# Attention scores in four groups of 32 rows on four PSUM banks, row maxima from the f32r tiles, another order of a step

## What is computed

```python
# layer 0: 16 heads of 16
Q = x @ Wq + bq
KV = text_input @ Wkv + bkv
scores = einsum('bqhd,bkhd->bhqk', Q, K) * 0.25
out = einsum('bhqk,bkhd->bqhd', softmax(scores, axis=-1), V)
# layer 1: 8 heads of 32
scores = einsum('bqhd,bkhd->bhqk', qh, kh) / 16
oh = qh + einsum('bhqk,bkhd->bqhd', softmax(scores, axis=-1), vh)
O = layernorm(oh); O = O + relu(O @ Wo.T + bo); O = layernorm(O)
```

## Time and profile before

| | us |
|---|---|
| median of 3 runs | 2231.89 |
| lowest, highest | 2225.58, 2285.02 |
| the profiled execution | 2223.33 |
| its span | 2221.6 |
| PE busy in the span | 1721.6 (77%) |
| DVE busy | 1030.7 (46%) |
| POOL busy | 1033.6 (47%) |
| ACT busy | 896.1 (40%) |

### The profile page before, as it was taken

The page is one execution under the profiler, slowest core; times in us unless marked ns, Lnnn a source line. Parts: engine busy times, 40 slices in busy tenths (PEclk is TensorE's granted clock), DMA queues, the critical chain, the costliest instruction groups (busy, mean ns, idle before and its releaser), DMA issues. The chain is left out here.

```text
span 2221.6 us, 45766 instructions
## 1 busy us (share of the span) xinstructions
PE 1721.6 (77%) x14350; PEld 1272.6 (57%) x14351; DVE 1030.7 (46%) x2291; ACT 896.1 (40%) x1823; POOL 1033.6 (47%) x1421
## 2 busy tenths in 40 slices
PE   5888888888864999958777777777775268888884
PEld 4666666666643666646666565656664135555552
DVE  3555555555534222224555555554455724444442
ACT  3666666666641222225444444444442011111110
POOL 4656666666631111134544555454543036666663
PEclk8999999999986999978989999999997589999998
DMA  4111111000014111120111111100000222222223
GB/s 111 41 46 59 44 63 44 26 26 19 20 31 163 33 33 33 33 73 12 51 40 61 47 48 41 48 23 27 25 23 12 94 80 36 38 38 38 38 38 81
DMA packets 54163, 102.08 MB, mean 46 GB/s; under 512 B 11842, under 2 KB 37674, under 8 KB 50698
## 3 DMA queue, kind: packets, MB, share of 16 engines
q1 hardware_dynamic: 37754, 78.87, 11.0%
q0 software_dynamic: 16352, 22.47, 5.5%
HBM read 79.78 MB, written 24.93 MB: 47 GB/s over the span
## 5 line engine op out<-in xcount | busy, mean ns | idle before, releaser
L950 DVE TENSOR_REDUCE a_mx<-a_SM 100x2 bf16<-100x722 f32 x384 | 350.2, 912 | 351.1 <-PE a_SM L423 349.2
L1533 PE MATMUL e_PH<-w,e_xT 128*128 x712 | 326.5, 602 | 6.0 <-DVE e_ab L1665 2.9
L695 ACT ACTIVATE a_Pr<-a_ST 120x800 f32<-120x800 f32 (+1 forms) x288 | 241.8, 854 | 46.6 <-PE a_ST L459 46.4
L423 PE MATMUL a_SM<-a_KTb,a_QMb 64*100 64x361 bf16 x768 | 136.9, 353 | 133.2 <-DVE a_mx L950 131.0
L745 POOL TENSOR_TENSOR a_rstd<-a_ve,a_powers 100x1 f32<-100x1 f32 x192 | 117.4, 611 | 223.2 <-DVE a_ve L919 223.1
L1533 PEld LDWEIGHTS e_PH<-w,e_xT 128*128 128x128 f32 x712 | 134.8, 193 | 141.4 <-issue 138.6
L1454 POOL COPY e_gidx<-toks 128x1 int32 (+1 forms) x89 | 48.6, 546 | 300.2 <-PE e_PX L1522 206.7
L470 PE MATMUL a_M<-a_Pr,a_V 120*32 120x100 f32 (+3 forms) x4608 | 186.6, 262 | 0.3 <-ACT a_Pr L695 0.3
L423 PEld LDWEIGHTS a_SM<-a_KTb,a_QMb 64*100 64x100 bf16 x768 | 47.0, 119 | 225.8 <-DVE a_mx L950 187.1
L1619 ACT ACTIVATE e_hT<-e_PT 128x512 f32<-128x512 f32 x57 | 34.0, 597 | 332.7 <-PE e_PY L1556 309.2
L452 PE MATMUL a_ST<-a_MXM,a_ones_bf 64*120 64x400 bf16 (+1 forms) x576 | 104.1, 357 | 68.3 <-POOL a_MXM L833 67.1
(11 more groups left out here) (194 smaller groups left out, 4038.2 us busy)
## 6 DMA issues: line engine op xcount, KB each, us to landing
w<-in_E_w SPq DMA_DIRECT2D x24, 1024.0 KB, 5.9
a_ct<-in_ctx SPq DMA_DIRECT2D x64, 362.0 KB, 3.2
keep_rows<-a_keep SPq DMA_DIRECT2D x64, 100.0 KB
tile_rows<-e_y SPq DMA_DIRECT2D x32, 128.0 KB
b_rows<-in_E_b SPq DMA_DIRECT2D x1, 4096.0 KB
sums<-X SPq DMA_DIRECT2D x1, 3200.0 KB
out<-sums SPq DMA_DIRECT2D x2, 1600.0 KB, 9.4
X<-in_x SPq DMA_DIRECT2D x1, 2800.0 KB
```

The source lines that it names most:

```text
L423: last = nc.tensor.matmul(SM[0:LQ, half, 0:LK], QMb[rows, chunk, m, :], KTb[rows, chunk, :], start=True, stop=True)
L695: nc.scalar.activation(dst.rearrange("p (j q) -> p j q", j=2), ST[0:n, (b.p * NS + s) % 2, :, 0:4 * LQ], ACT.Exp, scale=SCALE).then_inc(ex ...
L950: V_.tensor_reduce(pair, SM[0:LQ, :, 0:LK], AX_X, ALU.max).then_inc(max_done, 1)
L1533: last = nc.tensor.matmul(PH[:, h, :], xT[:, c, :], rhs, start=(c == 0), stop=(c == DC - 1))
```

## The change

- `ROWS` is 32 in both layers. In layer 0 HT becomes 2, in layer 1 it becomes 1: no mask and no spreading. There QM is written by ScalarE from the queries (in the place of q_hi), QL by GpSimd as queries minus QM, and MXM is the copy of the maxima that ScalarE makes.
- A slot is a key tile with all heads: three slots in both layers. Its products run over four row groups, each with its own bank of `ST`, which has four banks and one buffer. Slot s waits for the exponential of slot s-1. In layer 0 ScalarE's exponential is one instruction of 1600 columns.
- `score_rows` multiplies QM and KT; KTb and QMb with their copies are gone, and KF, KT and KL are 362 wide.
- The product with V runs by key tile (three blocks of all heads) and not by head group (four blocks of three tiles).
- In layer 1 the query rows are transposed from qf instead of being projected again.
- The order of a step changes on four engines: the front's first half stands ahead of the transposed maxima; VectorE's `tail1a` and `tail1c` stand ahead of all reduces; GpSimd's `power(2)` moves from ahead of the gather to the next step's start.

```diff
-TILE_ROWS = (64, 64)
+ROWS = 32
+GROUPS = 128 // ROWS
...
-        MXM = sb("MXM", [128, DC, HT, LQ], BF16)
+        MXM = sb("MXM", [128, DC, HT, LQ], BF16) if layer == 0 else mxT[:].unsqueeze(2)
...
-        ST = ctx.enter_context(nc.psum_tensor(tag + "ST", [128, 2, 2, 512], F32))
+        ST = ctx.enter_context(nc.psum_tensor(tag + "ST", [128, GROUPS, 512], F32))
...
                 if layer == 1:
                     for c in range(DC):
-                        last = nc.tensor.matmul(M0[0:LQ, D:2 * D], xT[:, c, :], wq[:, c, :],
-                                                start=(c == 0), stop=(c == DC - 1))
+                        last = nc.tensor.transpose(M0[0:LQ, D + c * 128:D + (c + 1) * 128], qf[:, c, :], ident[:])
...
                 for half in range(2):
-                    rows, chunk, m = place(j // 4 * 8 + half * 4 + j % 4)
-                    last = nc.tensor.matmul(SM[0:LQ, half, 0:LK], QMb[rows, chunk, m, :], KTb[rows, chunk, :],
+                    rows, chunk, m = place(half * NP + j)
+                    last = nc.tensor.matmul(SM[0:LQ, half, 0:LKP], QM[b.p][rows, chunk, m, :], KT[b.p][rows, chunk, :],
                                             start=True, stop=True)
...
-                if b.low >= 1 or s >= 2:
-                    pe.wait_ge(exp_done, b.count(NS, s - 1))
-                C = DC // EIGHTS
-                for j in range(2):
-                    rows = place(8 * eight + 4 * j)[0]
-                    nc.tensor.matmul(ST[0:n, buf, j, 0:4 * LQ], ones_bf[rows, 0:n],
-                                     MXM[rows, C * eight:C * eight + C, :, :], start=True, stop=False)
+                if b.low >= 1 or s >= 1:
+                    pe.wait_ge(exp_done, b.count(NS, s))
+                for r in range(GROUPS):
+                    rows = place(PER * r)[0]
+                    nc.tensor.matmul(ST[0:n, r, 0:PER * LQ], ones_bf[rows, 0:n], MXM[rows, :, :, :],
+                                     start=True, stop=False)
 
                 for k, (K, Q) in enumerate(((KT[b.p], QM[b.p]), (KT[b.p], QL), (KL[b.p], QM[b.p]))):
-                    for t in range(0, 4, HT):
-                        for j in range(2):
-                            rows, chunk, _ = place(8 * eight + 4 * j + t)
-                            last = nc.tensor.matmul(ST[0:n, buf, j, t * LQ:(t + HT) * LQ], K[rows, chunk, k0:k0 + n],
-                                                    Q[rows, chunk, :, :], start=False, stop=(k == 2 and t + HT == 4))
+                    for t in range(0, PER, HT):
+                        for r in range(GROUPS):
+                            rows, chunk, _ = place(PER * r + t)
+                            last = nc.tensor.matmul(ST[0:n, r, t * LQ:(t + HT) * LQ], K[rows, chunk, k0:k0 + n],
+                                                    Q[rows, chunk, :, :], start=False, stop=(k == 2 and t + HT == PER))
...
+                if fr:
+                    front(nxt)
                 if back:
                     max_columns(b)
                 if fr:
-                    front(nxt)
+                    project(nxt)
                 if back:
                     scores(b, 0)
...
                 if tail:
                     residual(prev)
                     residual_stats(prev)
+                    tail1a(prev)
+                    tail1c(prev)
                 for j in range(NP):
                     if fr:
                         maxima(nxt, j)
-                    if tail and j == 0:
-                        tail1a(prev)
-                        tail1c(prev)
```

More of the change, by code:

```diff
@@ L126, in attention @@
     NP = H // 2
[L127 to L129 removed]
+    NS = 3
     SCALE = 0.25 if layer == 0 else 1.0 / 16.0
@@ L526, in step @@
                 if fr:
-                    front(nxt)
+                    project(nxt)
                 if back:
                     scores(b, 0)
-                if fr:
-                    front_end(nxt)
-                pair = 0
-                for s in range(NS):
-                    if back:
-                        if s == 4:
-                            pe.wait_ge(exp_done, b.count(NS, 3))
-                            free_m0(nxt, fr)
-                            values(b, 0)
-                        if s > 0:
-                            scores(b, s)
-                    if fr:
-                        score_rows(nxt, pair)
-                        pair += 1
-                    if tail and s == 2 + (1 - layer):
-                        if fr:
-                            pe.wait_ge(v_evac, nxt.count(2, 1))
-                        out_transposes(prev, layer == 1, prev.low >= LAG)
@@ L548, in step @@
-                for g in range(EARLY, NG):
-                    if back:
-                        late = g == max(EARLY, EARLY_EXPS)
-                        if late:
-                            pe.wait_ge(exp_done, b.count(NS, NS - 1))
-                        if g == 0:
-                            free_m0(nxt, fr)
-                        last = values(b, g, late)
-                    if tail and g == 1:
-                        out_product(prev, layer == 1, prev.low >= LAG)
-                    if fr and layer == 0 and g == 2:
-                        score_rows(nxt, 6)
@@ L560, in step @@
-                if back:
-                    last.then_inc(av_ps, 1)
+                rows_of(*((0, 1), (0,))[layer])
+                if back:
+                    scores(b, 1)
+                if tail:
+                    if fr:
+                        pe.wait_ge(v_evac, nxt.count(2, 1))
+                    out_transposes(prev, layer == 1, prev.low >= LAG)
+                rows_of(*((2,), (1,))[layer])
+                if back:
+                    free_m0(nxt, fr)
+                    values(b, 0)
@@ new lines, in step @@
+                rows_of(*((3,), ())[layer])
+                if back:
+                    scores(b, 2)
+                rows_of(*((), (2,))[layer])
+                if back:
+                    values(b, 1)
+                rows_of(*((4,), ())[layer])
+                if tail:
+                    out_product(prev, layer == 1, prev.low >= LAG)
+                rows_of(*((5,), ())[layer])
+                if back:
+                    values(b, 2).then_inc(av_ps, 1)
+                rows_of(*((6,), ())[layer])
@@ L845, in step @@
                 ends = layer == 1 and tail and prev2.low >= 0
-                if back:
-                    for e in range(EIGHTS):
-                        masked_max(b, e)
+                if back and layer == 0:
+                    masked_max(b)
+                if ends:
+                    power(2, prev2)
                 if tail and layer == 0:
                     attended(prev)
+                if tail:
                     power(1, prev)
@@ L853, in step @@
                     low_parts(nxt)
-                if tail and layer == 1:
-                    power(1, prev)
                 if ends:
                     residual1(prev2)
-                if fr and layer == 0:
-                    masked_low(nxt, 0)
                 if ahead:
@@ L873, in step @@
                     query_bias(nxt)
-                if tail and layer == 1:
-                    power(2, prev)
                 if ahead and layer == 1 and nxt2.low + 1 < NB:
@@ L898, in _ @@
             if layer == 1:
+                power(2, fixed(NB - 1))
                 residual1(fixed(NB - 1))
```

191 lines of the change are left out of this document (88 added, 103 removed).

## The result

The changed kernel takes 2116.6 us, the median of four runs from 2101.2 to 2138.7, against 2258.0 (2225.6 to 2285.0) for the kernel before on the same chip. Two of the four executions before and one after ran slow at a lower clock, so the ratio given is that of the fast ones: 0.947, with a 95% interval from 0.934 to 0.961. So the kernel is faster, but by about half of what was forecast: the median lies above the forecast's own range (1960 to 2030) and just above the outer end of 2110. The profiled execution is the fastest of the four: 2101.2 us. It stands against 2223.3 before, which is what the sum was made against.

The account below looks back on a forecast made before the run. Layer 0 was taken as nearly bound by TensorE in alternation with VectorE, layer 1 by waits. 2223 less 46 (steps 19.31 to 17.8) less 183 (22.20 to 16.3) gave 1994, said as 1995 us, range 1960 to 2030.

Parts of the forecast that it names:

- outer end of 2110: Whole kernel: top of the wider range, 1945 to 2110, holding all but part of the second, first and fifth case.
- A set of four at 0.105: Scores, both layers: four matmuls on four row groups cost 0.105 us, as much as a pair.
- the 0.137 weighed against it: Scores: cost of a set by the skill page's 3.07 times; 0.6 us a step, 36 us if none hidden, 2030.
- The slot: Layer 0's scores of one key tile, all 16 heads: 0.17 + 6 x 0.105 + 0.15 = 0.95 us.
- The front's move: Layer 0: next sequence's transposes and six K products go ahead of the transposed maxima, 1.3 us moved.
- two instructions of about 0.5: Layer 1, VectorE: last sequence's tail moved ahead of the first reduce, about 0.5 us each, ready at 5.15.
- both arrive together: Layer 1: VectorE and the first rows (4.7 + 0.45) are both ready for the first reduce at 5.15 us.
- Rival 3: Layer 0's clock falls as TensorE is less busy: 1.46 us a step, 45 us, 2040 in all; chance 0.1.
- granted clock 1.00 in both: Sign in the new profile: TensorE at full clock in both layers; 23 of layer 1's 183 us are the clock's.
- Rivals 1 and 2: Scores: row groups overlap two by two (2103 us, chance 0.13) or not at all (2420 us, chance 0.03).
- rival 4: Layer 1's wait returns on GpSimd or the context's load: 2 to 3 us a step, 2060 to 2090; chance 0.06.
- three signs that would make the prediction wrong: Layer 1's step above 19 us, ScalarE's 1600-element call over 2, or layer 0's clock below 0.9.

Follow-up runs that it names:

- experiment 6: The changed kernel with the maxima's transposition ahead of the front's transposes and K products again, in both layers: 2119.2 us, ratio 0.949.
- x3: The changed kernel with, in layer 1, GpSimd's low parts ahead of its power and six unread products at each of two places: 2011.9 us, 0.903.
- x11: The changed kernel with only layer 1's KL subtracted by GpSimd in two halves: 2121.7 us, 0.956.
- experiment 7: x3 without the unread products ahead of layer 1's output transposes: 2048.3 us, 0.920.
- x2: The changed kernel with unread products in layer 1, six ahead of scores 1 and twelve ahead of the output transposes: 2028.7 us, 0.909.
- x1: The changed kernel with GpSimd's low part of K ahead of its power(1) in layer 1: 2070.4 us, 0.927.
- x6: x5 plus six unread products a step in layer 0, between rows 0 and rows 1: 2011.4 us, 0.902.
- x9: x3 with layer 1's KL subtracted by GpSimd in two halves and six unread products a step in layer 0: 2001.1 us, 0.899.
- x4: The changed kernel with VectorE's old order in layer 1, tail1a and tail1c behind the first reduce: 2100.8 us, 0.940.
- experiment 5: The kernel before the change with 16 and 19 unread products a step in layer 1's two long TensorE gaps: 2198.9 us, 0.985.
- x10: x3 with layer 1's unread products only between rows 0 and scores 1 (the same run as experiment 7): 2048.3 us, 0.920.
- x5: x3 with layer 1's KL made by VectorE behind its third reduce, and five unread products at each place: 2035.7 us, 0.913.

## Why the prediction was wrong in size and right in direction

**What bounds it, and the sum's frame: right,** but for a little. All of the change lies in the steps. I had taken layer 1's length from two steps, 22.20; over 27 it was 22.50.

**Layer 0: right, and its parts nearly so.** A set of four at 0.105 is exact, and the 0.137 weighed against it falls. That was 4/3.07 of a pair's 0.105, taken for the cost of one matmul; what one alone costs stands in no row here, so the ratio itself is not tested. The slot took 0.84 (410.37 to 411.21), not 0.95; the first rows stand at 4.11, not 4.4; the seven intervals took 11.09, not 11.35, with the 1600-element exponential at 1.51 (said 1.6) and the residual's transposes waiting 0.28 (said 0.5); the end took 2.02, not 2.05. That is 17.22 instead of 17.8. The front's move, 1.3 and 1.0 net, was 1.0 net in experiment 6. The three long steps took back (17.58 less 17.19) x 31 = 12 us.

**Layer 1: two steps failed.** The first is "then two instructions of about 0.5", with the "both arrive together" that rests on it; the second, and by the table the larger one, is the clock at 1.00, told below. The duration was read where GpSimd was doing nothing alongside. But the change moves L982 to ahead of the first reduce, and GpSimd's queue there has the power it waits for and right behind it KL, 1.7 us long. The power's end releases both at once. I had read GpSimd's order for its own lateness only, and never asked what else runs during VectorE's two instructions. L982 took 1.4 more than priced, and the loop's turn, which the sum didn't have, 0.82 in some steps (every second one in x3). The first reduce came at 7.82 and not at 5.15.

I did not use a rule that bears on this. The Trainium skill, page "SBUF — State Buffer", section "Who interferes with whom", says that a VectorE instruction with two inputs in SBUF contends with a GpSimd instruction that reads SBUF; and it says, of VectorE's two-port modes, that whoever issues first has the shared ports for the whole instruction. The trace agrees in L982 (0.48 alone, 1.87 against KL), in x3's sum with a_qtok (0.42 and 1.72), and in the reduces, whose one input is PSUM: 0.91 throughout. Most of x11 does not fit it, since two instructions of GpSimd, and not one, were waited for.

**The clock: the rival was named, but for the wrong layer.** Rival 3 gave layer 0 a fall and put its price at 1.46 a step; for layer 1 the forecast had "granted clock 1.00 in both" and booked 23 us of gain from it. Instead it fell to 0.79. My reason was that the clock fell after waits of 2.25 and 2.52 us, which the change shortens or removes. The step above has no gap over 1.40: three of 0.74, 1.40 and 0.59, 2.7 us together, stand ahead of the fall, and in experiment 7 shorter ones. And the fill of x2 shows the direction: with more work and nothing else changed, the clock is 1.00 and the step shorter by 2.66, of the 4.0 that layer 1 lacks.

**The sum again, with what was found.** Layer 1's forecast of 16.3 is what x3's shorter step takes, 16.34 (1192.03 to 1208.37), in which the rest of KL still holds one VectorE instruction (1.05 instead of 0.48): first reduce at 5.83 (said 5.15), last rows at 14.33 (said 13.9). From there, by the runs: 16.36, plus 0.80 for the loop's turn and the hold in every second step (x3's mean 17.16), plus 1.58 for the clock (x1, 18.74), plus 1.56 for the main hold and the clock that it takes along, is the 20.30 measured, 4.0 more than 16.3. The split of the last two depends on the order: by way of x2 the same 3.14 is 0.48 for the hold and 2.66 for the clock. That is 4.0 x 31 = 124 us. The 0.3 by which layer 1 before was longer than my two steps gives 9 back, and layer 0, where the step fell by 1.76 and not 1.5, gives 8: 1994 + 124 - 9 - 8 = 2101, the time of the profiled execution. It has to come out so, since the steps are the measured ones; what it shows is that nothing outside the steps is missing.

**The rivals.** Rivals 1 and 2 (row groups overlapping two by two or not at all) fall by the row of 0.105. Of rival 4 a small part came: ScalarE's split of the context (L595) waits for its load in eight of the 27 steps, 9.8 us together or 0.36 a step, and up to 1.60. Of the three signs that would make the prediction wrong, one appeared, a step of layer 1 above 19.

**Open.** What starts the half clock in layer 0's few long steps is not known. In the changed kernel (21.5 and 22.1 us) TensorE's waits ahead of it are those of every other step, the longest 1.01. The fill of layer 0 is no cure: x6 with it has a clock of 1.00 there, but so have x3 and x11 without it, and x9 with it has one step of 20.3. Nor do I know why VectorE was let in between GpSimd's halves in x9 and in one step of x11 but not in its others, or what each of layer 1's three short gaps contributes beyond experiment 7.

## What to carry to other kernels

When an instruction of VectorE is moved, look at what GpSimd runs at its new place, not only at what it waits for: with both inputs in SBUF it was held (L982, by KL) until the end of a long instruction of GpSimd, and one releaser (here the power) can start both at once. When the held instruction is moved away or GpSimd's order is changed, look which other one meets the long instruction then: in x1, x3 and x4 a part of the hold went to a neighbour. Where a change makes a step denser but leaves several short waits of TensorE close together, the clock is a term of the sum in that layer too, and a variant with unread products in the gaps shows in one run what it is worth. A good arrangement may be masked by such terms: with them mostly out of the way (x3, x9) this one gave 10%, not 5%, of which the kernel before would get 1.5% by unread products alone (experiment 5).

## What the runs showed of the hardware

- A set of four matmuls on four row groups of 32 rows costs 0.105 us, as a set of two on row groups of 64 did. In layer 1 it is the same with 100 columns as in layer 0 with 200 (1263.43 to 1263.64 for eight matmuls).
- A VectorE instruction held by GpSimd grew from 0.48 to 1.87 us, 0.42 to 1.72; cutting GpSimd's instruction in two let VectorE in after the first half in x9 (0.94) and in one step of x11 (1.11), but not in x11's other steps (2.01).
- The clock fell to 1.2 GHz for 6.6 us after gaps of 0.74, 1.40 and 0.59, and in x10 for 10.2 us after gaps of 0.40 and 0.57, where I had thought gaps of over 2 us were needed. Six and twelve more products a step brought layer 1 from 0.79 to 1.00 (x2).
- The subtraction of 128x724 took GpSimd 1.74 us and VectorE 0.90 (30 of 32 in x5).
